# Gated cross-attention with routed experts: tiles of two 128-row halves, weights by SyncE transfers, transposes at the end of the next slot, projection in quarters

## The reference

```
latents = layernorm(x)
q       = (layernorm(latents) @ Wq + bq) * 128 ** -0.5      # per batch, 8 heads
k, v    = concat([layernorm(ctx), layernorm(latents)]) @ Wkv + bkv
attn    = softmax(q @ k.T) @ v                              # 64 x 128 scores a head
x       = x + tanh(g_xattn) * (attn @ Wo + bo)
n       = layernorm(x)
p       = softmax(n @ Wr + br); take the 2 largest of 8
y_e     = relu(n @ W1[e] + b1[e]) @ W2[e] + b2[e]           # 128 -> 256 -> 128
x       = x + tanh(g_ffn) * sum over the 2 of p_e * y_e
```

## Time and profile before

| what | value |
|---|---|
| three runs, median (lowest, highest) | 934.15 us (928.44, 934.85) |
| profiled execution: its time, and the span of its instructions | 935.25 us, 933.2 us |
| busy: PE, PEld, DVE, ACT, POOL | 799.6, 601.6, 601.1, 514.2, 491.7 us |
| mean granted TensorE clock | 0.964 of full speed |
| chain that ended last: PE, DVE, ACT, issue, POOL | 64%, 10%, 7%, 6%, 5% |
| HBM read, written | 39.74 MB, 45.35 MB |

### The profile page before, as it was taken

How to read it: one execution, slowest core, us unless ns; L and a number is a source line. 1 busy time by engine, 2 the same in 40 slices (tenths; PEclk the granted TensorE clock), 3 DMA queues, 4 the chain that set the end, 5 groups by cost and what they waited for, 6 DMA issues and landing times.

```text
span 933.2 us, 15854 instructions
## 1 busy us (share of the span) xinstructions
PE 799.6 (86%) x4481; PEld 601.6 (64%) x4481; DVE 601.1 (64%) x1908; ACT 514.2 (55%) x1655; POOL 491.7 (53%) x510
## 2 busy tenths in 40 slices
PE   4757888788999898999899999989999989878750
PEld 4635556464778665777767686858587857568650
DVE  3515474846676947696958576868686758476661
ACT  3447566565757556666647575737575736334320
POOL 2103235253636347675344575747575756577555
PEclk9979999999999999999999999999999999989995
DMA  4963233102122112141212223322322222246552
GB/s 128 381 181 140 80 139 122 51 29 57 52 74 63 52 40 74 52 114 57 76 39 58 63 76 84 86 73 63 86 80 70 80 57 72 74 135 170 158 145 62
DMA packets 113976, 86.14 MB, mean 92 GB/s; under 512 B 11985, under 2 KB 104418, under 8 KB 113890
## 3 DMA queue, kind: packets, MB, share of 16 engines
q1 hardware_dynamic: 99618, 49.32, 19.1%
q0 software_dynamic: 8192, 16.79, 6.2%
q10 hardware_dynamic: 6080, 19.02, 5.1%
HBM read 39.74 MB, written 45.35 MB: 91 GB/s over the span
## 4 chain that ended last, share of the span: by engine, by line
PE 64%; DVE 10%; ACT 7%; issue 6%; POOL 5%; SPq 5%; DMA 3%; POOLq 0%; ACTq 0%; DVEq 0%
PE shared L1080 12%; PE batch L1049 11%; PE batch L1030 9%; PE hid_ps L1010 7%; PE y_ps L1019 6%; PE batch L1038 4%; ACT probs L601 3%; POOL yg L504 3%; PE shared L956 3%; PE shared L954 3%; PE shared L955 3%; ACT pT_sb L609 2%; DVE hs L915 2%; PE xt_ps L999 2%; SPq L394 1%
## 5 line engine op out<-in xcount | busy, mean ns | idle before, releaser
L546 POOL TENSOR_TENSOR probs<-probs,rsums 128x512 f32<-128x512 f32 x128 | 134.6, 1051 | 290.7 <-DVE rsums L909 289.4
L621 ACT ACTIVATE oT<-batch 128x512 f32<-128x512 f32 x128 | 76.6, 598 | 210.4 <-PE shared L1080 115.7
L601 ACT ACTIVATE probs<-batch,neg_max 128x128 f32<-128x128 f32 x512 | 180.9, 374 | 8.0 <-DVE neg_max L903 8.0
L903 DVE TENSOR_REDUCE neg_max<-batch 128x4 f32<-128x512 f32 x128 | 88.1, 688 | 120.1 <-PE batch L1030 118.9
L1049 PE MATMUL batch<-pT_sb,kvn 128*128 128x512 f32 x256 | 140.7, 631 | 24.4 <-ACT pT_sb L609 24.1
L1030 PE MATMUL batch<-kvT,qT 128*128 128x128 f32 x1024 | 142.9, 284 | 17.4 <-ACT oT L621 17.4
L1030 PEld LDWEIGHTS batch<-kvT,qT 128*128 128x128 f32 x1024 | 130.4, 195 | 42.0 <-ACT oT L621 28.7
L504 POOL DMA_INDIRECT yg<-sorted_y,home x128 | 126.5, 988 | 47.7 <-issue 31.9
L491 POOL DMA_INDIRECT sorted_x<-xn,row_of x128 | 130.9, 1023 | 32.3 <-issue 32.3
L1080 PE MATMUL shared<-oT,M 128*128 128x512 f32 x256 | 120.6, 615 | 0.8 <-ACT oT L621 0.8
L601 ACT ACTIVATION_READ_ACCUMULATOR probs<-batch,neg_max 128x1 f32 x512 | 110.1, 215 | 0.0
(11 more groups left out here) (138 smaller groups left out, 1256.2 us busy)
## 6 DMA issues: line engine op xcount, KB each, us to landing
sorted_x<-yg ACTq DMA_DIRECT2D x36, 512.0 KB, 3.6
xt<-sorted_x SPq DMA_DIRECT2D x106, 128.0 KB
sorted_y<-y_sb SPq DMA_DIRECT2D x106, 128.0 KB
kv<-in_ctx_dram SPq DMA_DIRECT2D x16, 256.0 KB, 3.7
kv<-in_x_dram SPq DMA_DIRECT2D x16, 256.0 KB, 4.2
xres<-in_x_dram SPq DMA_DIRECT2D x16, 256.0 KB, 3.0
out_dram<-x SPq DMA_DIRECT2D x16, 256.0 KB
sorted_x<-xn,row_of POOLq DMA_INDIRECT x128, 2.4
```

Source lines behind the costliest of these rows:

```text
L546: nc.gpsimd.tensor_tensor(pv, pv, rsums[:, m % 2, :].unsqueeze(2).broadcast_to([P, 4, P]), ALU.mult).then_inc(probs_ready, 1)
L601: last = nc.scalar.activation(probs[:, m % 2, c * P:(c + 1) * P], batch_ps[m % 3][:, c * P:(c + 1) * P], ACT.Exp, bias=neg_max[:, m % 2, c ...
```

## The change

- **Tiles of two halves.** A table entry is now a run of 128 rows of one expert, and a tile is two entries, which may be of different experts. 12 or 16 tiles a chunk, 88 in all, in slots 34 to 45, 58 to 73, 82 to 97, 106 to 121 and 130 to 157; no place is left out. `hidden_tile` is 4 matmuls of 128 columns where it was 2 of 256. `wt` holds two sets of weights a tile. The last combine is in slot 171.
- **Weights.** For tiles below slot 131 (61 of them) SP issues two SBUF-to-SBUF transfers of 128 x 642 floats (321 KB each) in place of POOL's copy; later ones are two ACT copies in place of one. Rows of `xt` come in two transfers. SP reads the table for rows and for experts, every four tiles.
- **The bias** `b1` enters as `max(h, -b1)`: one DVE instruction of 128x512 for two of 128x256. The missing `b1 @ W2` is added to `b2` once (`fold_biases`, slots 10 to 13).
- **Order.** `TURN = 1`: PE transposes the probabilities of batch `n-1` after `output_tile` in slot `n`, with only place "c" behind them, and ACT copies them late in the slot. `OUT = 2`: the product of batch `n-2` is PE's second piece. POOL multiplies first in its slot.
- **Projection.** Four quarters of 8 matmuls with 128 columns, `oT` as the weights, in s=4, 6 of the group and s=0, 2 after it. DVE reads each quarter straight into `x1` (scale, and `xres` to which POOL has added the bias); the copy to `yT` and the `residual` transposes go.
- **Moved by a slot.** Of DVE's work: measuring the rows s=3 to s=1 and 2, their normalisation s=4 to 3, ranking s=7 to 6, placing and listing s=1 to 0 (and ahead of the context's normalisation). Queries, router and the table move with them.

```diff
-TILE = 256
-J = ROWS // TILE
-TILES = tuple((2 * c * TOK + E * (TILE - 1)) // TILE for c in CHUNKS)
...
+HALF = 128
+TILE = 2 * HALF
+J = ROWS // HALF
+HALVES = tuple((2 * c * TOK + E * (HALF - 1)) // HALF for c in CHUNKS)
+TILES = tuple((m + 1) // 2 for m in HALVES)
...
-PACK = 2 * D + 2 * D + 2 + D
...
+USED = 2 * D + 2 + D
+PACK = USED + 2 * D
...
-EXP, TURN = 1, 2
+EXP, TURN, OUT = 1, 1, 2
...
-AT_ONCE = 8
...
+AT_ONCE = 4
...
-        n = max(n, GB * (LAST_GROUP[k] + 2) + 7 + AHEAD)
+        n = max(n, GB * (LAST_GROUP[k] + 2) + 6 + AHEAD)
         for _ in range(TILES[k]):
-            while n < B + GB and n % GB == 2:
-                n += 1
...
-            if n % GB in (0, 1, 2, 7) or n > GB * (G + 1) + 6:
+            if n % GB in (0, 1, 6, 7) or n > GB * (G + 1) + 5:
...
-    0: [("turn_kv", 1, 0, "a"), ("place", -2, 0, "b")],
-    1: [("turn_kv", 1, 1, "a"), ("table", -2, 0, "c")],
-    2: [("project", -1, 0, "ab")],
-    3: [("residual", -1, 0, "a"), ("query", 1, 0, "b"), ("query", 1, 1, "c")],
-    4: [("query", 1, 2, "a"), ("query", 1, 3, "b"), ("query", 1, 4, "c")],
-    5: [("turn_x", -1, 0, "a"), ("query", 1, 5, "b"), ("query", 1, 6, "c")],
-    6: [("router", -1, 0, "a"), ("query", 1, 7, "b")],
+    0: [("project", -1, 2, "a"), ("table", -2, 0, "c")],
+    1: [("turn_kv", 1, 0, "a"), ("turn_kv", 1, 1, "b")],
+    2: [("project", -1, 3, "a")],
+    3: [("query", 1, 0, "a"), ("query", 1, 1, "b"), ("query", 1, 2, "c")],
+    4: [("project", 0, 0, "a"), ("turn_x", -1, 0, "b")],
+    5: [("router", -1, 0, "a"), ("query", 1, 3, "b"), ("query", 1, 4, "c")],
+    6: [("project", 0, 1, "a"), ("query", 1, 5, "b")],
+    7: [("query", 1, 6, "a"), ("query", 1, 7, "b"), ("place", -1, 0, "c")],
...
+        wt = sb("wt", [P, WB, 2, PACK])
+        hs = sb("hs", [P, 2, 2, 2, HALF])
...
                 wait(sp, xt_ready, i - XB + 1)
-                sp.dma_start(xt[:, i % XB, :, :], xs[k % SETS][bass.ds(first_rows[i], TILE), :].rearrange("(a p) d -> p a d", a=2)).then_inc(got_x[i % XB], 16)
+                for a in range(2):
+                    sp.dma_start(xt[:, i % XB, a, :], xs[k % SETS][bass.ds(first_rows[i, a], HALF), :]).then_inc(got_x[i % XB], 16)
...
+            def fetch_weights(i):
+                k = CHUNK_OF_TILE[i]
+                t = i - FIRST_TILE[k]
+                if i == 0:
+                    sp.wait_ge(experts_ready, 1)
+                if t % AT_ONCE == 0:
+                    read_table(mybir.EngineType.SP, 1, experts, i, LATE, E - 1)
+                wait(sp, y_done, i - WB + 1)
+                for a in range(2):
+                    sp.dma_start(wt[:, i % WB, a, :], wall[:, bass.ds(experts[i, a], 1), :].rearrange("p e n -> p (e n)")).then_inc(wt_early[i % WB], 16)
...
                     store_tile(TILE_AT[n - 2])
+                if TILE_AT.get(n + 1, N_TILES) < LATE:
+                    fetch_weights(TILE_AT[n + 1])
                 if n + AHEAD in TILE_AT:
...
+                for half in range(2):
+                    g = (n + 1 - 4 * half) // GB
+                    if s == (7, 3)[half] and 0 <= g < G:
+                        at = slice(g * GB + 4 * half, g * GB + 4 * half + 4)
+                        wait_shared(sp, shared_out, "project", g - 1, 2 * half + 1)
+                        sp.dma_start(xres[:, 2 * half:2 * half + 2, :],
+                                     x[at, :, :].rearrange("(c b) s d -> (b s) c d", b=2)).then_inc(got_xres[half], 16)
...
                 m = n - EXP
                 if 0 <= m < B:
                     pool.wait_ge(rsum_ready, m + 1)
...
-                if TILE_AT.get(n + 1, N_TILES) < LATE:
-                    fetch_weights(TILE_AT[n + 1])
+                for half in range(2):
+                    g = n // GB
+                    if s == (1, 5)[half] and 0 <= g < G:
+                        if g == 0:
...
+                        pool.wait_ge(got_xres[half], 16 * (g + 1))
+                        mine = xres[:, 2 * half:2 * half + 2, :]
+                        nc.gpsimd.tensor_tensor(mine, mine, bo_rows[:, :].unsqueeze(1).broadcast_to([P, 2, D]),
+                                                ALU.add).then_inc(xres_ready[half], 1)
+                g = n // GB - 2
+                if 2 <= s <= 5 and 0 <= g < G:
+                    scatter_rows(g, s - 2)
+                if n in GATHER_AT:
+                    gather_rows(*GATHER_AT[n])
+                g = n // GB - 1
+                if s == 2 and 0 <= g < G:
+                    pool.wait_ge(mv1_done, 2 * (g + 1))
+                    nc.gpsimd.tensor_tensor(rstd1[:, :], var_eps1[:, :], neg_half[:, 0:4], ALU.pow).then_inc(rstd1_done, 1)
+                g = (n - AGGREGATE) // GB
+                if s == AGGREGATE % GB and 0 <= g < G:
+                    pool.wait_ge(mv_done, 2 * (g + 1))
+                    nc.gpsimd.tensor_tensor(rstd[:, :], var_eps[:, :], neg_half[:, :], ALU.pow).then_inc(rstd_done, 1)
...
                                                     ACT.Exp, bias=neg_max[:, m % 2, c:c + 1],
                                                     accum_out=sums[:, m % 2, c:c + 1])
                     last.then_inc(exp_done, 1)
-                m = n - TURN
+                m = n - OUT
                 if 0 <= m < B:
-                    act.wait_ge(pT_ready, m + 1)
-                    wait(act, o_ready, m)
-                    nc.scalar.activation(pT_sb[:, :], batch_ps[m % 3][:, :], ACT.Copy).then_inc(pT_done, 1)
+                    act.wait_ge(o_ready, m + 1)
+                    g, b = m // GB, m % GB
+                    if b % 2 == 0:
+                        wait_shared(act, shared_full, "project", g - 1, b // 2)
+                    nc.scalar.activation(oT[:, :, b * L:(b + 1) * L], batch_ps[m % 3][:, :].rearrange("p (h i) -> p h i", h=H),
+                                         ACT.Copy).then_inc(o_out, 1)
                 g = n // GB - 1
...
+                if s == 6 and 0 <= g < G:
                     act.wait_ge(route_step, ROUTE * g + 2)
...
-                if 0 <= m < B:
-                    act.wait_ge(o_ready, m + 1)
-                    if m % GB == 0:
-                        wait_shared(act, shared_full, "project", m // GB - 1, 0)
-                    b = m % GB
-                    nc.scalar.activation(oT[:, :, b * L:(b + 1) * L], batch_ps[m % 3][:, :].rearrange("p (h i) -> p h i", h=H),
-                                         ACT.Copy).then_inc(o_out, 1)
...
+                m = n - TURN
+                if 0 <= m < B:
+                    act.wait_ge(pT_ready, m + 1)
+                    wait(act, o_ready, m)
+                    nc.scalar.activation(pT_sb[:, :], batch_ps[m % 3][:, :], ACT.Copy).then_inc(pT_done, 1)
...
-                nc.scalar.activation(wt[:, i % WB, :], wall[:, bass.ds(experts[i], 1), :].rearrange("p e n -> p (e n)"),
-                                     ACT.Copy).then_inc(wt_late, 1)
+                for a in range(2):
+                    last = nc.scalar.activation(wt[:, i % WB, a, :], wall[:, bass.ds(experts[i, a], 1), :].rearrange("p e n -> p (e n)"),
+                                                ACT.Copy)
+                last.then_inc(wt_late, 1)
...
-                    for c in range(2):
-                        last = nc.vector.tensor_scalar(hs[:, i % 2, c, :], hid(i)[:, c * TILE:(c + 1) * TILE],
-                                                       wt[:, i % WB, 4 * D + c:4 * D + c + 1], 0.0, ALU.add, ALU.max)
-                    last.then_inc(hs_done, 1)
+                    nc.vector.tensor_tensor(hs[:, i % 2, :, :, :], hid(i)[:, :].rearrange("p (a c j) -> p a c j", a=2, c=2),
+                                            wt[:, i % WB, :, 2 * D:2 * D + 2].unsqueeze(3).broadcast_to([P, 2, 2, HALF]),
+                                            ALU.max).then_inc(hs_done, 1)
+                for what, g, number, bank in shared_at(n, "a", "dve"):
+                    if what == "project":
+                        wait_shared(dve, shared_full, "project", g, number)
+                        dve.wait_ge(xres_ready[number // 2], g + 1)
+                        nc.vector.scalar_tensor_tensor(out=x1[:, g, number, :], in0=shared[bank][:, 0:D], scalar=tg[:, 0:1],
+                                                       in1=xres[:, number, :], op0=ALU.mult, op1=ALU.add).then_inc(shared_out[bank], 1)
+                place_rows(n, s)
+                list_tiles(n, s)
+                keep_table(n, s)
                 split_latents(n, s)
-                for what, g, number, bank in shared_at(n, "a", "dve"):
-                    if what == "residual":
-                        wait_shared(dve, shared_full, "residual", g, 0)
-                        dve.wait_ge(got_xres, 16 * (g + 1))
-                        nc.vector.tensor_tensor(x1[:, g, :, :], shared[bank][:, :].rearrange("p (c d) -> p c d", c=4),
-                                                xres[:, :, :], ALU.add).then_inc(shared_out[bank], 1)
...
```

(36 more changed lines are left out.)

179 lines of the change are left out of this document (83 added, 96 removed).

## The result

| | before | after |
|---|---|---|
| median of 4 runs (lowest, highest) | 934.5 us (928.44, 936.27) | 943.82 us (939.8, 952.39) |
| profiled execution, span | 935.25, 933.2 us | 942.63, 940.8 us |
| first to last scores of the attention | 37.0 to 791.1: 754.1 us | 41.6 to 812.6: 771.0 us |
| from there to the end | 142.1 us | 128.2 us |

The ratio is 1.0138, 95% interval 1.0099 to 1.0177: **slower by 1.4%**, where 1.3% faster was forecast. The part behind the attention gained 14 us, the attention itself lost 17, and its first scores come 4.6 us later.

A forecast was written before the change was run, and what follows sets the result against it. DVE's in-order work in the loop to the transposes was to pace the attention; 800 us to slot 130's tile plus 51, 7 and 63 gave a 921 us span, 922 on the median's scale; range (8 in 10) 885 to 953.

The forecast's parts named there:

- Weights by SP: Tiles in the attention: transfers of 4.0 us a pair, late in some slots, 8 us over 60 tiles, half counted: 4.
- The rival with late weights: Tiles in the attention: at 6.3 us a pair, weights come late and the kernel takes 955 us; chance 0.18.
- DVE inside the loop: Attention: DVE's in-order work delays the transposes; groups without tiles take 42.6 us, groups with tiles 50.0.
- the last part of the prediction: Signs: without tiles POOL waits for `rsums` and PE's transposes for POOL, longest in s=7, s=1, s=3; groups 42 to 44 us.
- The table: DVE's listing, moved to s=0, stands before the context and next `rsums`: 3.7 us each time, 22 in all.
- Quarters: Projection on PE: a quarter is 16 instructions, 1.78 us; four matmuls of 128 columns cost 0.89.
- The start: Start of the attention: first scores at 37 us and group 0 at 45, as before.
- Behind the attention: After slot 130's tile: tiles at 2.15 us, fifth chunk 51 us, then 7, then 63 of gathers, combining and stores.
- PE paces the attention: Rival: DVE reads quarters early enough, groups take 48.7 us with tiles and 36 without, 861 in all; chance 0.15.
- POOL holds the loop: Rival: POOL's scatters and gathers delay the loop 1 us in each of 14 groups, 936 us, no change; chance 0.17.

The follow-up runs named there:

- E1: Changed kernel with SP reading the experts' table one slot earlier, behind that slot's transfers: 973.0 us, on a chip where the changed kernel took 988.08.
- E6: Changed kernel with the changes of E1 and E2 at once: 938.25 us, ratio 0.9542 to the kernel before on the same chip.
- E2: Changed kernel with DVE's normalising of the next context's first four batches moved from s=6 to s=7: 954.87 us, where the changed kernel took 988.08.
- E8: Changed kernel with the changes of E1, E2 and E3 together: 884.25 us, ratio 0.9459 to the kernel before on the same chip.
- E3: Changed kernel with the probabilities' transposes, their ACT copy and the product back at the old places: 957.27 us, where the changed kernel took 988.08.

## Why the prediction was wrong

922 us were forecast and 943.82 measured. The attention ends 24 us later than forecast (817.9 for 794, to slot 128), what is behind it takes 4 less. Of the 24, 15.6 lie in the four groups in which SP reads late (5, 8, 11 and 14: 217.8 us for 198.2, less the 4 counted for late weights), 8.4 in the other four with tiles, six in each (4, 7, 10 and 13: 201.0 for 192.6); what is left is at most 4 us a part and cancels.

**The step that failed first is "Weights by SP", a term of the sum: 4 us, where removing it gave 15 (E1) and 17 (E6 less E2).** Its mechanism was right and was named: SP issues late behind `y_sb`, latest where it reads the table. The reading was 1.8 us by estimate and is 2.6 (3.11 less 0.52). There were not 2 us to spare in s=1: with the reading gone (E1) the weights of slots 42, 66, 90 and 114 are used 3.61 to 3.85 us after their first issue, just in time, so with it PE waits for them 11.7 us. The prediction's 8 us does not say how many tiles are late; four at its 2 us give it. And I halved the sum because others would hide it; on the contrary it grew to 17 us of longer slots, by the low clock behind each wait (1.7 us in slot 90). The pair of transfers itself was about right at 4.0 us: in the four long waits PE went on 3.53, 3.57, 4.83 and 4.55 us after the first issue, with the DMA engines at 0.92 in the third, slot 90. The Trainium skill, DMA: Bandwidth & Descriptors, Anatomy of one DMA, had given an estimate of 3.5 us for the pair, by figures for transfers that GpSimd issues, where here SP does; the trace agrees in slots 42 and 66 (3.53 and 3.57), not in the two others. The rival with late weights had the right place and sign; it asked for 6.3 us a pair and gave 955.

**The second is the clock behind PE's waits, for which the sum had no term.** The attention was to take as long as before. With tiles DVE was to be late by 0.7 us in s=7, and it is (6.38 us, 5.78 in E2). But groups 4 and 10, which have no long wait for weights, took 51.5 and 52.0 us, where 42.6 + 6 x 0.93 is 48.2. In E2, without the wait of 3.1 us ahead of them, they take 47.5 and 47.6: their slots s=0 went from 6.5 us at a granted clock of 0.61 to 4.06 and 4.85 at 1.00. Over the whole attention the granted clock was 0.98 before, 0.96 in the changed kernel and 0.99 in E8. The prediction priced each wait at its own length.

**DVE inside the loop: right in mechanism and, without tiles, in size.** Tile-less groups were to take 42.6; group 2 took 41.4 and group 1 44.0. PE waited for POOL in s=7, s=1 and s=3, longest in s=7, 3.1 us, as the last part of the prediction asked; these slots of group 2 take 7.09, 6.11 and 5.78 us for 6.7, 6.3 and 5.8. The total is in part luck: s=4 to s=6 take 14.4 us together for 15.6, for neither the 5.4 of PE nor POOL's 6.0 shows in any of them. What I did not ask was what the group would take if only the transposes stayed: E3's 38.2. The forecast compared the new loop with the old loop of the old kernel (43.9), so that a choice that costs 31 us looked neutral. That was an omission in reading the change part by part, not a wrong number. Nor did I ask what the context was still doing in s=6 once the ranking had come there: E2's one line gains 33.

**The table: right.** Four groups at +3.7; groups 3, 6, 9 and 12 took 47.1, 46.8, 48.8 and 49.8, with two tiles in each of the last two: 0.5 to 1.6 above 46.3 and 48.2.

**Quarters: right.** A quarter of 16 instructions starts 1.79 us before the next piece (541.06 to 542.85), forecast 1.78, and four matmuls of 128 columns cost 0.89 (540.17 to 541.06), as forecast.

**The start: right as a sum.** First scores at 41.6 for 37, group 0 in 38.4 for 45; group 1 begins at 80.0 us, forecast 82.

**Behind the attention: right.** 14 us less than before where 12 were forecast: the step to the tile of slot 130 is 7.8 us (817.9 to 825.66, forecast 6), tiles take 2.1 to 2.4 there (they start at 866.57, 868.68, 870.90, 873.32), and from that tile to the end it is 115.1 us, forecast 121.

*PE paces the attention* is out: groups 1 and 2 took 44.0 and 41.4 us, not 36, and PE waited 51.3 us for POOL. *POOL holds the loop* is out for the changed kernel: `rsums` ended POOL's wait 117 times in 128.

## What to carry to other kernels

When a change has several parts, price each against the change without it, not against the kernel before: a part that loses 31 us can look neutral because another part paid for it. When work moves closer to its producers, look at what else those producers do in that slot: moving one line of it (E2) gained as much as taking the move back (E3). An engine's queue that only issues transfers is still an in-order queue: a reading of numbers into registers stands ahead of the transfer behind it, and costs per number, so it belongs in a slot where nothing is due. And a wait of PE is worth more than its own length when the clock drops behind it.

## What the hardware showed

- **Two kinds of chip, one program.** On the two chips of B the kernel before is 48 us slower than on A; on the one of them on which it was profiled none of that is in the attention. Behind it, two lines of the waits from 787 us on, on B:

```profile
ACT wt L652 <- DVE y_sb L943: 49.1, 14, 9.5
ACT wt L652 <- issue: 43.2, 12, 15.5
```

  On A the same copy waited 2.2 us, once, without a named releaser. Two stretches of B's profile, as windows:

```profile
830.00:880.00 50.00, 31.35 (x155) 25.79 (x155) 20.10 (x65) 12.24 (x24) 23.11 (x24) 0.70 0.33 95
880.00:930.00 50.00, 31.87 (x193) 28.75 (x192) 24.07 (x66) 13.27 (x27) 16.08 (x17) 0.80 0.37 105
```

  On A the granted clock was 0.93 from 830 to 880. PE was busy 31 of 50 us on B and 41 on A, so the low clock goes with the waits; which of the two comes first, and why ACT stands still for up to 15.5 us with nothing named, stays open.
- **Registers.** On SP a reading of 4, 8 or 16 numbers costs 0.30, 0.52 or 1.22 us for the load and 0.25 us for each number behind it.
- **The clock.** After 3.64 us without work PE's granted clock was 0.61 over the next 4.4 us, and 1.00 behind them. From 211.40 to 215.80, behind the wait of 3.09 us, it was 0.50, the lower of the chip's two levels (1.2 and 2.4 GHz), and the scores took 1.85 us for 0.89. A wait of 3.1 us does not always do it: behind those ahead of groups 2 and 7 the clock stayed at 1.00.
